# Decoder layer with routed experts on one core: weight conversion moved from the head of the attention stage to its tail, three hand-written orders, loop written out

## What is computed

```python
x = layernorm(x + attention(x, Wq, Wk, Wv, Wo, bo))      # 16 heads of 8, softmax
x = layernorm(x + retention(Q=x, K=ctx, V=ctx))          # 16 heads, xpos rotation, decay, causal
x = layernorm(x + experts(x, gate, w1, w3, w2))          # 8 experts, top 2, silu(x w1) * (x w3) @ w2
```

## Time and profile before

| | |
|---|---|
| median of three runs | 1058.34 us (1056.09 to 1058.72) |
| profiled execution, its own time | 1065.84 us |
| its span, first to last instruction | 1063.7 us |
| mean granted TensorE clock | 0.903 |
| busy, share of the span | PE 80%, DVE 75%, POOL 61%, ACT 58% |
| last count of stage A on DVE | 655.4 us |
| first load of stage B on SP | 672.8 us |

### The profile page before, as it was taken

One profiled execution on the slowest core, in us unless ns is written; L12 is line 12 of the kernel. 1 busy time (PEld: TensorE's weight loads), 2 busy tenths in 40 slices (PEclk: granted clock), 3 DMA queues, 4 the chain that ended last, 5 costly groups with the idle time before them and its releaser, 6 DMA issues.

```text
span 1063.7 us, 36375 instructions
## 1 busy us (share of the span) xinstructions
PE 856.2 (80%) x12164; PEld 640.8 (60%) x12165; DVE 800.6 (75%) x2219; ACT 621.2 (58%) x1416; POOL 650.5 (61%) x738
## 2 busy tenths in 40 slices
PE   1573969899999899898987871599999999999600
PEld 1352546666567566565655541488888888888600
DVE  3776779999789788797765653588887888777565
ACT  1032446677667666676566862466666666666445
POOL 0353756699989989899777546144444444444443
PEclk9685989999999999999889975799999999999855
DMA  6223211222212313222121101222122112122076
GB/s 231 61 52 83 55 36 39 51 62 53 68 47 62 72 40 71 49 51 61 32 53 50 35 29 61 63 62 57 56 60 59 58 57 58 56 60 57 33 254 220
DMA packets 145252, 72.10 MB, mean 68 GB/s; under 512 B 75024, under 2 KB 134544, under 8 KB 145136
## 3 DMA queue, kind: packets, MB, share of 16 engines
q1 hardware_dynamic: 124800, 40.56, 16.3%
q0 software_dynamic: 8640, 17.84, 5.0%
q10 hardware_dynamic: 11696, 12.08, 3.5%
HBM read 42.11 MB, written 28.34 MB: 66 GB/s over the span
## 4 chain that ended last, share of the span: by engine, by line
PE 36%; POOL 7%; issue 5%; DMA 3%; DVE 3%; ACT 2%; SPq 1%; another core or an unknown queue 0%; POOLq 0%; ACTq 0%; DVEq 0%
PE QKV L770 9%; PE ST L770 9%; PE XT L798 5%; PE SC L798 5%; POOL prod_ev L1550 4%; POOL routed_rows L1567 2%; DMA prod_ev<-token_halves 2%; PE ST L640 1%; ACT q L923 1%; PE YY L788 1%; PE ST L655 1%; PE TR L788 1%; PE YY L588 1%; POOL rs L1530 1%; DMA routed_rows<-xe,pos 1%
## 5 line engine op out<-in xcount | busy, mean ns | idle before, releaser
L1550 POOL TENSOR_TENSOR prod_ev<-e_sb,q_v 128x512 f32<-128x512 f32 x256 | 295.9, 1190 | 101.3 <-PE YY L588 61.6
L1599 POOL DMA_INDIRECT token_halves<-w_new,tok_i x142 | 137.9, 971 | 39.4 <-issue 33.6
L1567 POOL DMA_INDIRECT routed_rows<-xe,pos x128 | 131.4, 1026 | 30.4 <-issue 29.4
L1150 DVE TENSOR_TENSOR prod_qk<-q_v,QKV 128x2048 f32<-128x2048 f32 x64 | 145.4, 2274 | 0.0
L1036 ACT ACTIVATE prod_qk<-QKV,silu_scale 128x512 f32<-128x512 f32 x142 | 95.9, 687 | 61.5 <-PE QKV L770 60.0
L1452 DVE TENSOR_TENSOR prod_ev<-prod_qk,prod_ev 128x1024 f16<-128x1024 f32 x71 | 87.0, 1225 | 54.2 <-ACT prod_ev L1027 34.4
L770 PE MATMUL QKV<-k_t,w_hl 128*128 128x256 f16 x852 | 117.1, 274 | 0.1
L770 PE MATMUL ST<-k_t,w_hl 128*128 128x256 f16 x852 | 117.0, 274 | 0.1
L411 POOL TENSOR_TENSOR marks<-half_c 128x1 f32<-128x1 f32 x103 | 19.9, 193 | 151.1 <-DVE w_new L1468 150.9
L1478 DVE SCALAR_TENSOR_TENSOR prod_qk<-ST,hid_scale,prod_qk 128x512 f32<-128x512 f32 x142 | 102.4, 744 | 10.1 <-ACT prod_qk L1036 7.1
L923 ACT ACTIVATE q<-XT,tab 128x256 f32<-128x256 f32 x256 | 96.6, 497 | 0.0
(11 more groups left out here) (169 smaller groups left out, 1791.9 us busy)
## 6 DMA issues: line engine op xcount, KB each, us to landing
w_new<-routed_rows SPq DMA_DIRECT2D x71, 130.0 KB
prod_ev<-token_halves SPq DMA_DIRECT2D x16, 512.0 KB, 5.0
x_sb<-x SPq DMA_DIRECT2D x32, 128.0 KB, 2.6
x_res<-x SPq DMA_DIRECT2D x128, 32.0 KB
head_rows<-o_n SPq DMA_DIRECT2D x32, 128.0 KB
o_t<-head_rows SPq DMA_DIRECT2D x64, 64.0 KB
ctx_sb<-ctx SPq DMA_DIRECT2D x32, 128.0 KB
out<-prod_qk ACTq DMA_DIRECT2D x16, 256.0 KB, 4.4
```

Of the source, the lines that this page charges most:

```text
L1150: eng.tensor_tensor(prod_qk[:, u, :, :].rearrange("p d (i j) -> p d i j", j=NH), q.unsqueeze(3).to_broadcast([P, HD, NH, NH]), k.unsqueeze ...
L1550: ins = eng.tensor_tensor(prod_ev[:, u, q, :, :, 0:HD], e_sb[:, it.slot(2), u, 64 * q:64 * q + 64].rearrange("p (i j) -> p j i", j=4).unsq ...
L1567: eng.indirect_dma_start(out=xs, out_offset=bass.IndirectOffsetOnAxis(ap=pos[:, r, 2 * u + k:2 * u + k + 1], axis=0), in_=xe[:, r, u, k, : ...
L1599: eng.indirect_dma_start(out=halves, out_offset=bass.IndirectOffsetOnAxis(ap=tok_i[:, s, u:u + 1], axis=0), in_=yw[:, s, u, :], in_offset= ...
```

## The change

1. `A_FIRST` becomes 32 = the number of duos, so the loop is gone: all steps are written out.
2. `run_steps` takes three bodies: `fill` for the first 13 steps, `step` for the others up to 31, `drain` for those after. Each engine but SP has its own three orders, and the lags are others.
3. The middle order of TensorE begins with `ret_values`, takes `scores` one step later than `project` (lag 3, not 2), and runs `residual` and `project` between the two retention scores' waits. On POOL the first scatter of a duo comes a step earlier (lag 10, not 11). On DVE all lags are counted from `products` = 0.
4. The weights leave steps 0 to 9. Only w1's load is issued at the start. `measure(0)` stands in DVE's step 31, and the rest in the drain, tied to how far the last duo is. All three go through `w_new`, so w3 is loaded after w1's low part and w2 after w3's. The wait of the first `queries_across` copies on `lo_ready` goes.
5. The blank rows for padding are in `prod_ev`, written by POOL after the last `sums`.
6. `wait_last`, which waits for the last of several readers of a shared PSUM buffer, waits for all of them in steps where two orders meet.

```diff
-def run_steps(eng, n, first, lags, body):
+def run_steps(eng, n, first, lags, body, fill=None, drain=None, n_fill=0):
...
     for s in range(first):
-        alone(s)
+        alone(s, fill if s < n_fill else body, 0 < n_fill and not n_fill + 4 <= s < n - 3)
...
     for s in range(n, n + lags):
-        alone(s)
+        alone(s, drain or body, drain is not None)
...
-    A_FIRST = 20
-    PE_LAGS, ACT_LAGS, DVE_LAGS, POOL_LAGS, SP_LAGS = 13, 13, 14, 11, 9
-    CTX_LAG, HEADS_LAG = 9, 8
+    A_FIRST = 32
+    PE_LAGS, ACT_LAGS, DVE_LAGS, POOL_LAGS, SP_LAGS = 15, 19, 20, 11, 7
+    CTX_LAG, HEADS_LAG = 7, 6
+    N_FILL = 13
...
-        pad_rows = zero_rows(w_new)
+        pad_rows = zero_rows(prod_ev[:, :, :, :, :, :].rearrange("p u q j i d -> p (u q j i d)"))
...
             def load_weights(n):
 
+                if n > 0:
+                    eng.wait_ge(lo_ready, n)
                 if n < 2:
-                    eng.dma_start(fresh(n).rearrange("p (e i) -> p e i", e=n_exp),
+                    eng.dma_start(w_new[:, :].rearrange("p (e i) -> p e i", e=n_exp),
                                   (w1, w3)[n].rearrange("e h i -> h e i")).then_inc(w_in[n], 16)
...
-                if it.i is None and it.off < 2:
-                    eng.wait_ge(lo_ready, 2)
...
+            def drain(at):
+                if last(at, 9):
+                    high(1)
+                if it := at(9):
+                    queries_across(it)
...
+                if last(at, 3):
+                    load_weights(1)
...
+                if last(at, 9):
+                    load_weights(2)
+                if last(at, 19):
+                    high(2)
...
+                if it := at(9):
+                    ret_across(it)
+                if last(at, 2):
+                    high(0)
```

628 lines of the change are left out of this document (460 added, 168 removed).

## The result

The changed kernel took 1075.18 us (median of 14 executions, 1061.24 to 1086.45), the kernel before 1060.7 on the same chip (14 executions): ratio 1.0098, 95% interval 1.0065 to 1.0132. It is slower by 1%. (Medians go over all executions, ratios in this document only over those within 1.5% of the fastest one of the same kernel; here that leaves out six of the changed kernel's 14, and the two medians alone would give 1.0137.) The prediction said 1025 us, 1000 to 1046, and gave slower a chance of 0.07. Its profiled execution took 1073.74 us, span 1071.9, against 1065.84 and 1063.7 before.

What follows compares the result with a forecast made beforehand. It took stage A as deciding: weight waits in the filling, TensorE (busy 176.4 of 189 us) and loop boundaries in the middle, retention in the emptying. -45 - 8.3 + 19.7 = -33.6 from 1058.34 gave 1025 us, range 1000 to 1046.

Steps and rivals of the forecast that it cites:

- Term 1: Filling, start to duo 12's copy: weight work and landing waits leave it, 208 to 163 us, -45.
- The walk: Filling: the new order followed duo by duo, first copy near 18 us, then twelve pitches totalling 145.
- Rival 4: Filling: its steps are their own chain, not held by the weights, so only -15, total 1055; chance 0.08.
- Term 2: Middle, duo 12 to duo 31: without the loop 19 steps of 16.3 us, 309.7 against 318.0, -8.3.
- the circle: Middle: chain from mask 1 through DVE's queries, q copies, residual and scores back to mask 1, 16.3 us per duo.
- The rule of the lock: DVE instructions with two SBUF inputs and POOL instructions reading SBUF exclude each other; weighed with w2's low part, 5.44 for 4.5.
- The loop's share: Middle: removing the loop's long boundary pitches, all else unchanged, would leave 15.8 us per duo, -17.8.
- Term 3: Emptying, duo 31's copy to stage B's first load: the weight work moved there costs +19.7 on 146.9 us.
- One routing step fewer lies between the second residual and the positions: Emptying: with this and the first scatter a step earlier, -4 us.
- Rival 3: Emptying: two low parts hold POOL 4 to 4.5 us each on the path, total 1034; chance 0.05.
- The signs set beforehand: Wrong if duo 12 after 180 us, middle pitch under 15.9 or over 16.8, or emptying over 175.
- Rival 5: Emptying: the three weights run one behind another in the open, 66 us, total 1071, slower; chance 0.06.

Runs made afterwards that it cites:

- a_wfill: Changed kernel with the weight conversion back in the filling, as in the kernel before, none in the emptying; 1150.62 us, ratio 1.104 to the kernel before.
- after_again: Changed kernel unaltered, run again as a control on chip 0; 1142.09 us, ratio 1.094 to the kernel before.
- a_resid: Changed kernel with TensorE's residual ahead of the q8-copy wait; 1050.47 us, ratio 0.992; repeated on chip 0: 1134.98, 1137.82 and 1025.26 us, no ratio.
- a_blocks: Changed kernel with ACT's two ctx_bd copies behind the eight q8 copies in the middle order; 1146.34 us, ratio 1.104 to the kernel before.
- ar_qb: ar_q with ACT's two ctx_bd copies also behind the q8 copies; 1028.21 us, ratio 0.983 to the kernel before.
- a_q: Changed kernel with DVE's query and key products ahead of the first score product in the middle order; 1050.51 us, ratio 1.005 to the kernel before.
- b_loop_out: Kernel before with only A_FIRST set from 20 to 32, so stage A has no hardware loop; 1050.91 us against 1060.05, ratio 0.990.
- ar_q_wfill: ar_q with the weight conversion back in the filling, as in the kernel before; 1060.92 us on chip 7, ratio 1.003 to the kernel before.
- a_nofill: Changed kernel with N_FILL 0 instead of 13, so the middle order runs from step 0; 1096.03 us, ratio 1.033 to the kernel before.
- a_scat11: Changed kernel with POOL's scatter 0 at lag 11, directly ahead of scatter 1, in all three orders; 1106.52 us, ratio 1.062 to the kernel before.
- ar_qsb: ar_qb with POOL's scatter 0 also at lag 11 beside scatter 1; 1081.35 us, ratio 1.036 to the kernel before.
- ar_q: Changed kernel with the edits of a_resid and a_q together; 1026.92 us, ratio 0.982; repeats 0.982 (1025.4 us) and 0.989 (chip 7).

## Why the prediction was wrong

**Term 1 (-45, measured -48.8)** came out, its reason only half. The walk itself held: its twelve pitches were put at 145 us and took 142.3. With the weights in the filling the new orders alone put duo 12 at 185.4, 22.6 under before; the weights gave the other 26.9 (both on another chip than the kernel before's trace; on chips 4 and 0 a_wfill and after_again give 24.5). Rival 4 fell.

**Term 2 (-8.3, measured +27.6)** is the step that failed, in three places.

1. *"then PE, which waits for them ahead of `residual`"*: the circle was drawn through DVE's queries, with nothing ahead of the `q` copies on ACT. The chain of waits of the changed kernel goes another way: retention values, `rt`, `ctx_bd`, `q`, `residual`, and then all of TensorE's step to the next retention values. By its rows that is 0.58 + 0.83 + 3.03 and hand-overs, 4.5, and 12.85 from `residual` (360.46 one step earlier) to the end of the retention values at 373.3: 17.35, the measured pitch. Out of it a_resid took `residual`, and the pitch fell to 16.6. `ctx_bd`'s was not shown: a_blocks ran on another kind of chip, and in ar_qb TensorE was the bound.
2. The 12.85 holds 1.2 us of the hole. Such stalls were in the kernel before too (46 late completions), but there, it seems, they fell where less waited for them; I took no account of them, since no row of a view shows them, only a wait of ACT or POOL longer than the product it waits for.
3. The rule of the lock was weighed for the low parts alone. The prediction cited it under *"A rule against this change"*, and did not ask which instructions of the middle it covers. The order of the changed kernel puts the query and key products, all with two SBUF inputs, behind the first score product, just where POOL is released by the sums. The excess of these four products over 0.42 us is 12.9 us in the middle of the changed kernel, 0.7 in the kernel before, and 78.5 in after_again. Against the 16.74 us per duo of the kernel before, the four slow steps (85.7 us) are 18.8 of the 27.6 us, and the fourteen others behind them, 17.4 on average, some 9. Against the even steps the four are 16 us too long, and some 5 of these are TensorE's own products at the lower clock (69.2 us busy against 64): the prediction has no term for the clock in the middle. a_q shows the cure for the slow steps on a chip with few late completions; on one with many it was not run.

The loop's share was mis-sized too: *"If nothing else changed, 19 duos at 15.8 would give 300.2, that is -17.8"*; b_loop_out measured -8.4.

**Term 3 (+19.7, measured +31.1).** The weights' part was right in sum, 22.4 measured against the 23.7 of its items, though not item by item. What was missing is some 11 that the orders cost without weights (157.9 in ar_q_wfill against 146.9; traces of the kernel before and of b_loop_out spread from 140.5 to 149.7). *"One routing step fewer lies between the second residual and the positions"*, put at -4, looked at the routing only: `residual`, the retention scores and the retention values each stand one step later behind `project` than before, so the emptying has a step more of retention. Part of term 1's gain is this same work, not yet done at duo 12. Behind the last count the prediction added the whole of w2's chain, +10.5, *"After that the scales and the tile table take the 17.5 us up to the first load as before"*. The chain did take 9.2, but the stretch grew only by 4.8, since POOL's indirect DMAs end last there; on that path it is the low part's hold on one of them that counts, 4.73 us instead of 0.96. Rival 3 (two low parts hold POOL) was thus right in kind and nearly in size: the hold of 3.8 and that on `nb`, 4.2, which the critical view passes through too, are 8 us of its 9.

The signs set beforehand did their work: duo 12 under 180, pitch over 16.8, over 175 us in the emptying. Rival 5, the one that ended slower, put 66 us into the emptying, which took 31.1; none had the middle above 17.1 us per duo, and it took 18.2.

**What stays open.** Why TensorE stalls on some chips and not on others. In before, changed, a_resid, a_nofill and b_loop_out, 229 of the 235 late completions come 0.2 to 1.3 us behind the end of one of POOL's indirect DMAs, at sums, scores or project alike; such moments are 24% of the time. But the pair issued beside the sums in after_again (at the same distance as in the changed kernel) brings none on chip 0. So the DMAs are tied to it and are not enough. That it is the chip, and not something else that differed between the sets, rests on five sets. The edit of a_scat11 was not tried on a chip with late completions, nor ar_qb, which would show the place of `ctx_bd` there, nor a_q. What puts a_resid into one regime or the other on chip 0 is open too.

## What to carry to other kernels

An order written out by hand is good only with the times that it was made for. Before trusting a pitch, list which DVE instructions with two SBUF inputs stand within reach of a group of POOL products, and put an instruction with a PSUM operand between them, so that a microsecond either way changes nothing (ar_qsb, where POOL comes later by its four DMAs, shows the limit): ar_q is 1.8% faster than the kernel before on two sets and 1.1% on a third, and the kernel it came from ran 1% slower on one chip and 9% on another. When two unrelated edits give the same bad number, run the unaltered kernel again beside them before explaining either.

## What the runs showed of the hardware

- Two SBUF inputs on DVE against POOL products that read SBUF: 0.42 us becomes 1.38 (a reading: the two take turns), or 5.1 to 5.5, which covers all four POOL products in a row (4.52). Both forms occur in one trace. A row of 1.38 costs POOL something too: four of its products took 5.34 beside them. The Trainium skill (SBUF — State Buffer, "SBUF: two separate sides") has the exclusive lock; these rows agree, and add that the loser may lose four turns running. With one operand in PSUM all 64 score products took 2.25 to 2.29 us, beside POOL as well as alone.
- The other way round: each of the three low parts (4.49 us, two SBUF inputs) held one POOL instruction, two indirect DMAs (4.80 and 4.73 us for 0.96) and `nb` (4.37 for 0.20). Beside the measure at 652.80 (4.41 us, one SBUF input) the indirect DMAs took 0.96 and 0.97.
- TensorE pays twice for a wait of some 5 us: in after_again the granted clock is 0.5 for 3.4 or 6.8 us in nearly every step of some 23 us, and the same products keep it busy for 330.5 us instead of the 291.7 of ar_q.
- Chips are not alike: on chips 5 and 7 and that of the first comparison TensorE's completions come up to 2.8 us late, two to four in a step on average, on chips 4 and 0 almost never; the kernel before is 12 to 18 us shorter on the latter. A ratio measured on one chip, 1.0098, was 1.094 on another.
